# Three kinds of fp32 matmuls issued as halves in two column tiles of TensorE, in a macaron block with a gated delta rule

## The chip, the cores and the metric

The kernel runs as one program on one core of a Trainium2 chip. The metric is the device time of that core in microseconds (us). TensorE does the matmuls: it holds a stationary operand (the weights, at most 128 rows by 128 columns) and streams a moving operand of up to 512 columns past it, and it writes to PSUM, which has eight banks of 512 fp32 columns over 128 partitions. VectorE, ScalarE and GpSimd take the results out of PSUM and work on them, and SyncE issues the transfers (DMA). Each engine runs its own instructions in order and waits for others by semaphores.

## The reference

The input `x` has 8 sequences (B) of 512 positions (T) and 128 features (D). Three layers follow one another, each added to `x`:

```
x = x + 0.5 * ffn(layernorm(x))          # gated feed-forward, hidden 512
x = x + attn(layernorm(x))
x = x + 0.5 * ffn(layernorm(x))          # the same weights again

attn:  n = layernorm(x);  q = l2norm(silu(n @ Wq)); k = l2norm(silu(n @ Wk)); v = silu(n @ Wv)   # 8 heads of 128
       beta = sigmoid(n @ Wb); alpha = sigmoid(n @ Wa)
       S_t = a_t (I - b_t k_t k_t^T) S_{t-1} + b_t k_t v_t^T ;  o_t = S_t^T q_t                   # over t, for each head
       x = x + o @ Wo;  x = x + gelu(layernorm(x) @ W1 + b1) @ W2 + b2
```

All of it is in fp32.

## The kernel before

The recurrence over 512 positions is cut into 4 chunks (NC) of 128 positions. Within a chunk the products of keys with keys, masked and decayed, give a triangular matrix whose inverse is built by blocks (32, then 64, then 128), and a state of 128 x 128 for each of the 8 heads is carried from chunk to chunk. The eight sequences go through a software pipeline, written out by hand for each engine: while sequence s goes through its four chunks with the state, the projections and keys with keys of sequence p = s + 1 and the feed-forward layers of their neighbours stand between its pieces in TensorE's queue. Nothing is scheduled by a planner: the order in which the functions are called in `SP_first`, `SP_step` and `SP_last` is the order on TensorE.

These pieces of TensorE's program matter here:

- `proj(b, c, i)`, L1384 to L1391: one of the six projections (halves of 4 heads of q, k and v) of a chunk: stationary is `nT`, 128 x 128, moving a slice of `wqkv`, 128 x 512; it fills one bank (4 or 5). One matmul.
- `keys_keys(b, c, g)`, L1402 to L1415: for 4 heads (g = 0 or 1) the 128 x 128 product of the keys with themselves; stationary and moving are both `KT`. Four matmuls in bank 6 or 7, one column range each.
- `state_keys(b, c, g)`, L1432 to L1438: for 4 heads the keys with the state; stationary `KT`, moving `state`, 128 x 128. Four matmuls in bank 0 or 1.
- `join_one`, L1698 to L1716, called by `join`: the block inverse. It works with 32 x 32 and 64 x 64 pieces that lie in other rows (SBUF partitions of the operands) and other columns (PSUM partitions of the result) of the array. `join` issues two sides in turn; side 0 writes to bank 6, side 1 to bank 7. In step 3 (L1715 and L1716) both sides read partitions 32 to 63, one writes to partitions 0 to 31 and one to 32 to 63. In steps 5 and 8 (L1706 alone, L1707 alone) both sides lie in the same 64 x 64 tile.
- Full-array matmuls around them: the feed-forward layers L1284 (512 moving columns) and L1292 (128), the solve L1446, the queries with the state L1463, the update L1454, the output L1473, the attention's output L1482. L1384 is a small product with 32 stationary and 128 moving columns, over all 128 rows.

One step of `SP_step` issues in this order: `state_keys`, 2 projections, `solve`, `state_queries`, `update`, `keys_keys`, 2 projections, `output`, 2 projections, `attend`. The first sequence has its own functions for projections and keys with keys (`proj0`, `keys_keys0`: L1582, L1611), which the change leaves alone.

Of the kernel before, what the change touches and what calls it, by code (L numbers as in the profile page):

```python
# [52 lines left out]
def place(b, c, i):  # L53

    return ALONE.index((c, i)) if b == 0 else 6 * c + STEP_ORDER.index(i)


def at_end(b, c):

    return (b, c) == (B - 1, NC - 1)  # L60


def build_program(nc, d):
# [3 lines left out]
    with ctx:  # L67
        def sb(name, shape, dt=f32):
            return ctx.enter_context(nc.sbuf_tensor(name, shape, dt))

        def sem(name):
            return ctx.enter_context(nc.semaphore(name))
# [7 lines left out]
        wqkv = sb("wqkv", [128, 3, H * 128])  # L80
# [28 lines left out]
        nT = sb("nT", [128, T])  # L109
# [15 lines left out]
        KT = sb("KT", [128, U, 128])  # L125
# [6 lines left out]
        state = sb("state", [128, H, 128])  # L132
# [34 lines left out]
        bank = [ctx.enter_context(nc.psum_tensor(f"bank{i}", [128, 512], f32)) for i in range(8)]  # L167

        def heads(bk):
            return bk[:, :].rearrange("p (h n) -> p h n", h=4)  # L170
# [70 lines left out]
        p_proj, p_silu = sem("p_proj"), sem("p_silu")  # L241
# [1032 lines left out]
        def _(pe):  # L1274
# [111 lines left out]
            def proj(b, c, i):  # L1386
                n = place(b, c, i)
                if n >= 2:
                    pe.wait_ge(p_silu, b * 6 * NC + n - 1)
                pe.matmul(bank[4 + n % 2][:, :], nT[:, 128 * c:128 * c + 128], wqkv[:, i // 2, 512 * (i % 2):512 * (i % 2) + 512],  # L1390
                          start=True, stop=True).then_inc(p_proj, 1)  # L1391

            def turn(b, c, g):

# [7 lines left out]
            def keys_keys(b, c, g):  # L1402

                if at_end(b, c):
                    pe.wait_ge(p_trc, 4 * NC + g + 1)
                elif g == 0:
                    pe.wait_ge(k_in[c % 2], 16 * NBLK * (2 * (b - 1) + c // 2 + 1))
                if c > 0:
                    pe.wait_ge(p_dk, b * 2 * NC + 2 * c - 1 + g)
                else:  # L1410
                    pe.wait_ge((j_dve, j_act)[g], b * NS)
                for h in range(4):
                    u = H * c + 4 * g + h
                    last = pe.matmul(heads(bank[6 + g])[:, h, :], KT[:, u, :], KT[:, u, :], start=True, stop=True)  # L1414
                last.then_inc(p_kk, 1)  # L1415

            def keys_queries(b, c, g):
# [14 lines left out]
            def state_keys(b, c, g):  # L1432

                pe.wait_ge(s_S, b * 6 + 2 * (c - 1) + g + 1)
                for h in range(4):
                    u = H * c + 4 * g + h
                    last = pe.matmul(heads(bank[g])[:, h, :], KT[:, u, :], state[:, 4 * g + h, :], start=True, stop=True)  # L1437
                last.then_inc(s_ks, 1)  # L1438

            def solve(b, c, g):  # L1440
# [44 lines left out]
            def SP_first(s, p):  # L1485

                pe.wait_ge(j_dve, s * NS + AHEAD)
                pe.wait_ge(j_act, s * NS + AHEAD)
                if p is not None:
                    pe.wait_ge(n_bias, s + 2)  # L1490
                solve(s, 0, 0), solve(s, 0, 1)
                early = p is None or p == 1
                if not early:
                    pe.wait_ge(F["f1"]["sc"], p + 1)
                    pe.wait_ge(F["f2"]["sc"], p)
                    proj(p, 0, 2), proj(p, 0, 3)
                join(s, AHEAD, JOIN_BANKS)
                update(s, 0, 0)
                if not early:
                    proj(p, 0, 0)  # L1500
                update(s, 0, 1)
                if not early:
                    proj(p, 0, 1)
                join_waits(s, AHEAD + 1)
                output(s, 0, 0), output(s, 0, 1)
                join(s, AHEAD + 1, JOIN_BANKS)
                if p is not None:
                    proj(p, 0, 4), proj(p, 0, 5)
                attend(s, 0)

            def SP_step(s, p, c, f1):

                state_keys(s, c, 0), state_keys(s, c, 1)
                if p is not None:
                    proj(p, c, 2), proj(p, c, 3)
                if c < 3:
                    pe.wait_ge(j_act, s * NS + AHEAD + c)
                    pe.wait_ge(j_dve, s * NS + AHEAD + c)
                solve(s, c, 0), solve(s, c, 1)
                state_queries(s, c, 0), state_queries(s, c, 1)  # L1520
                if c < NC - 1:
                    update(s, c, 0), update(s, c, 1)
                elif p is not None:
                    proj(p, c, 0), proj(p, c, 1)
                if p is not None:
                    keys_keys(p, c - 1, 0), keys_keys(p, c - 1, 1)
                if c < NC - 1 and p is not None:
                    proj(p, c, 0), proj(p, c, 1)
                output(s, c, 0), output(s, c, 1)
                if p is not None:  # L1530
                    proj(p, c, 4), proj(p, c, 5)
                    if c == NC - 1 and f1 is not None:
                        input_T("f1", f1)
                    if at_end(p, c):
                        turn(p, c, 0), turn(p, c, 1)
                attend(s, c)

            def SP_last(s, p, f1):

                if f1 is None and p is not None:  # L1540
                    keys_keys(p, NC - 1, 0), keys_keys(p, NC - 1, 1)
                if f1 is not None:
                    layer1("f1", f1, 0)
                    pe.wait_ge(s_xa, s * NC + NC)
                    layer1("f1", f1, 1), layer1("f1", f1, 2), layer1("f1", f1, 3)
                    keys_keys(p, NC - 1, 0), keys_keys(p, NC - 1, 1)
                    pe.wait_ge(F["f1"]["silu"], f1 * KB + 3)
                pe.wait_ge(ln_m.rows, s + 1)
                transposes(xa, m_tr)
                if f1 is not None:  # L1550
                    pe.wait_ge(p_silu, p * 6 * NC + 6 * NC)
                else:
                    pe.wait_ge(s_xa, s * NC + NC)
                    M_up(s, None), M_down(s, p)
                    if p is not None:
                        keys_queries(p, 0, 0), keys_queries(p, 0, 1)
# [230 lines left out]
```

## Time and profile before

| | |
|---|---|
| median of 2 runs | 1490.54 us (1488.46 to 1492.62) |
| the profiled execution, its own time | 1489.32 us |
| its span, first to last instruction | 1487.6 us |
| mean granted TensorE clock | 0.982 of full speed |
| TensorE busy | 1418.9 us (95%) |
| VectorE, ScalarE, GpSimd busy | 820.9 (55%), 668.6 (45%), 564.9 us (38%) |

The profile is of one execution. "PE" is TensorE's matmuls and "PEld" its weight loads, which can lie beneath matmuls; the recorded length of a matmul holds its way through the array, so it is longer than the distance from one to the next. The chain of waits goes back from the last instruction to what released it, each time; its pieces have the distances between instructions, not their recorded lengths. L1390 and the like are lines of the kernel. An engine's idle time counts only if it lies on that chain.

### The profile page before, as it was taken

Reading aid. Unit: us, or ns where it says so; the run is one execution under the profiler, and the core shown is the slowest. Engines: PE = TensorE matmul, PEld = TensorE weight load, DVE = VectorE, ACT = ScalarE, POOL = GpSimd, SP = SyncE. Lnnn points to the kernel's source line nnn. Section 1 sums busy time; section 2 is a strip of 40 time slices with the busy share of each in tenths; the row PEclk is TensorE's granted clock in tenths of the full one; section 3 lists DMA queues with packets and bytes.
Section 4 is the critical chain, followed back from the end, with each engine's and each line's share of the span. In section 5 each row is a group of like instructions: output and inputs, shape, how many; then the busy total and the mean of one; then the engine's idle time right before and its main releaser. Section 6 shows DMA issues by size and latency. Waiting matters only on the chain.

```text
span 1487.6 us, 25821 instructions
## 1 busy us (share of the span) xinstructions
PE 1418.9 (95%) x10118; PEld 966.2 (65%) x10118; DVE 820.9 (55%) x2432; ACT 668.6 (45%) x1130; POOL 564.9 (38%) x641
## 2 busy tenths in 40 slices
PE   7998899999999999999999999999999999889968
PEld 3455776557866587557865588566875578656934
DVE  3467387454865367644764557753776437641330
ACT  2466466225652356325562256523563256512222
POOL 0038042831447133650428314471336504381000
PEclk9999899999999999999999999999999999989979
DMA  5130244532454135630455325641356304543000
GB/s 173 42 100 29 41 104 116 108 82 65 122 115 99 34 88 130 132 82 23 104 123 102 82 65 122 111 106 31 92 126 124 82 23 111 112 77 76 1 0 7
DMA packets 359546, 125.04 MB, mean 84 GB/s; under 512 B 325280, under 2 KB 340352, under 8 KB 359424
## 3 DMA queue, kind: packets, MB, share of 16 engines
q1 hardware_dynamic: 359424, 123.38, 36.2%
q8 instruction: 80, 1.31, 0.3%
q14 instruction: 42, 0.34, 0.1%
HBM read 79.58 MB, written 43.76 MB: 83 GB/s over the span
## 4 chain that ended last, share of the span: by engine, by line
PE 89%; DVE 7%; ACT 1%; DMA 1%; SPq 1%; issue 1%; DVEq 0%; ACTq 0%
PE bank L1284 29%; PE bank L1390 9%; PE bank L1313 5%; PE bank L1292 4%; PE bank L1446 4%; PE bank L1473 4%; PE bank L1482 4%; PE bank L1429 3%; PE bank L1414 3%; PE bank L1454 3%; PE bank L1463 3%; PE bank L1437 3%; PE bank L1706 2%; PE bank L1671 2%; PE bank L1680 2%; PE bank L1715 1%
## 5 line engine op out<-in xcount | busy, mean ns | idle before, releaser
L1284 PE MATMUL bank<-big,h 128*128 128x512 f32 x992 | 447.1, 596 | 0.0
L1284 PEld LDWEIGHTS bank<-big,h 128*128 128x128 f32 x992 | 181.6, 190 | 197.0 <-issue 192.5
L512 POOL TENSOR_TENSOR rnorm<-ssq,mhalf 128x16 f32<-128x16 f32 (+1 forms) x35 | 84.0, 2401 | 516.8 <-DVE ssq L773 516.8
L1390 PE MATMUL bank<-wqkv,nT 128*128 128x512 f32 x336 | 160.2, 596 | 0.0
L558 POOL TENSOR_TENSOR blkT<-blkT,blkP 128x31 f32<-128x31 f32 (+15 forms) x248 | 135.8, 547 | 19.4
L555 POOL TENSOR_TENSOR blkP<-blkA,blkT 128x31 f32<-128x31 f32 (+15 forms) x248 | 129.2, 521 | 31.1 <-DMA blkA<-blocks_out 12.3
L1313 PE MATMUL bank<-xT,w 128*128 128x512 f32 x256 | 122.7, 626 | 8.4 <-ACT xT L1038 4.2
L908 DVE TENSOR_SCALAR TB<-bank 32x512 f32<-32x512 f32 (+1 forms) x48 | 33.1, 689 | 153.0 <-PE bank L1713 74.3
L1055 ACT ACTIVATE big<-bank,cols 128x512 f32<-128x512 f32 x64 | 43.0, 686 | 138.3 <-PE bank L1284 100.4
L887 DVE TENSOR_TENSOR MT<-bank,MT 128x512 f32<-128x512 f32 x56 | 38.6, 691 | 104.3 <-PE bank L1429 104.3
L1313 PEld LDWEIGHTS bank<-xT,w 128*128 128x128 f32 x256 | 49.0, 201 | 66.5 <-issue 50.9
L1062 ACT ACTIVATE big<-bank,cols 128x512 f32<-128x512 f32 x64 | 43.1, 686 | 108.6 <-PE bank L1284 108.5
L521 POOL TENSOR_TENSOR MT<-rows_or_g,maskf 128x1024 f32<-128x1024 f32 x28 | 78.2, 2792 | 11.5 <-PE bank L1473 11.0
L539 POOL TENSOR_TENSOR QET<-QET,sgf 128x1024 f32<-128x1024 f32 x21 | 49.3, 2350 | 86.7 <-DMA sgf<-e_rows 86.7
L1390 PEld LDWEIGHTS bank<-wqkv,nT 128*128 128x128 f32 x336 | 56.8, 191 | 37.4 <-issue 36.8
L1124 ACT ACTIVATE MT<-MT,biasj 128x128 f32<-128x128 f32 x256 | 78.2, 389 | 0.3
L1446 PEld LDWEIGHTS bank<-V,R 128*128 128x128 f32 x512 | 63.0, 196 | 15.0 <-issue 12.5
L1429 PEld LDWEIGHTS bank<-QET,KT 128*128 128x128 f32 x448 | 58.4, 197 | 20.4 <-issue 14.4
L1292 PE MATMUL bank<-w,big 128*128 128x128 f32 x512 | 68.2, 279 | 2.3 <-DVE TB L908 1.5
L1292 PEld LDWEIGHTS bank<-w,big 128*128 128x128 f32 x512 | 62.6, 192 | 11.8 <-issue 8.4
L1134 ACT ACTIVATE big<-bank 128x512 f32<-128x512 f32 x56 | 32.7, 597 | 82.8 <-PE bank L1390 82.7
L1446 PE MATMUL bank<-V,R 128*128 128x128 f32 x512 | 64.7, 281 | 3.7 <-DVE V L915 2.1
(213 smaller groups left out, 2598.6 us busy)
## 6 DMA issues: line engine op xcount, KB each, us to landing
rows_or_g<-g_rows SPq DMA_DIRECT2D x28, 512.0 KB, 4.9
q_rows<-mid SPq DMA_DIRECT2D x28, 512.0 KB, 4.9
QET<-q_rows SPq DMA_DIRECT2D x112, 128.0 KB, 4.2
k_rows<-R SPq DMA_DIRECT2D x27, 512.0 KB, 2.7
KT<-k_rows SPq DMA_DIRECT2D x108, 128.0 KB, 3.6
sgf<-e_rows SPq DMA_DIRECT2D x21, 512.0 KB, 4.6
blocks_out<-R SPq DMA_DIRECT2D x128, 32.0 KB, 1.7
blkA<-blocks_out SPq DMA_DIRECT2D x8, 512.0 KB, 3.8
```

The costliest lines, as they stand in the source:

```text
L512: pool.tensor_tensor(rnorm[:, heads_of], ssq[:, heads_of], mhalf[:, :].to_broadcast([128, heads_of.stop - heads_of.start]), ALU.pow).then_ ...
L521: pool.tensor_tensor(MT[:, u, :], grow, maskf[:, :].unsqueeze(1).to_broadcast([128, H, 128]), ALU.add).then_inc(d_mask, 1)
L555: pool.tensor_tensor(prod, A3[:, j, j + 1:].unsqueeze(2).to_broadcast([128, n, m]), T3[:, j:j + 1, 0:m].to_broadcast([128, n, m]), ALU.mul ...
L558: pool.tensor_tensor(T3[:, j + 1:, 0:m], T3[:, j + 1:, 0:m], prod, ALU.subtract).then_inc(b_prod, 1)
L1124: last = act.activation(MT[:, u, :], MT[:, u, :], ACT.Exp, bias=biasj[:, u:u + 1])
L1284: last = pe.matmul(bank[bk + i][:, :], w[:, k, 128 * o:128 * o + 128], src[:, k, :], start=(k == 0), stop=(k == KB - 1))
L1292: last = pe.matmul(bank[4][:, 128 * c:128 * c + 128], src[:, k, 128 * c:128 * c + 128], w[:, k, :], start=(k == 0 and c == 0), stop=(k == ...
L1313: pe.matmul(bank[bk][:, :], w[:, 128 * o:128 * o + 128], xT[:, :], start=True, stop=True).then_inc(f["gate"], 1)
L1390: pe.matmul(bank[4 + n % 2][:, :], nT[:, 128 * c:128 * c + 128], wqkv[:, i // 2, 512 * (i % 2):512 * (i % 2) + 512], start=True, stop=True ...
L1429: last = pe.matmul(heads(bank[6 + g])[:, h, :], KT[:, u, :], QET[:, u, :], start=True, stop=True)
L1446: last = pe.matmul(heads(bank[g])[:, h, :], R[:, u, :], V[:, u, :], start=True, stop=True)
L1473: last = pe.matmul(heads(bank[2 + g])[:, h, :], V[:, u, :], MT[:, u, :], start=(c == 0 and h == 0), stop=True, skip_group_check=True)
```

## The change

In `proj`, the 128 stationary columns are issued as two matmuls of 64 columns, the first writing to PSUM partitions 0 to 63 and the second to 64 to 127; the moving operand of 512 columns is streamed by both. `state_keys` is cut in the same way, in turn for each head. In `keys_keys` the stationary and the moving columns are both halved, so that each head has four matmuls of 64 x 64 with the two partition halves in turn. The semaphore is raised by the last matmul only, as before.

```diff
--- before.py
+++ after.py
@@ -1387,8 +1387,10 @@
                 n = place(b, c, i)
                 if n >= 2:
                     pe.wait_ge(p_silu, b * 6 * NC + n - 1)
-                pe.matmul(bank[4 + n % 2][:, :], nT[:, 128 * c:128 * c + 128], wqkv[:, i // 2, 512 * (i % 2):512 * (i % 2) + 512],
-                          start=True, stop=True).then_inc(p_proj, 1)
+                for half in (slice(0, 64), slice(64, 128)):
+                    last = pe.matmul(bank[4 + n % 2][half, :], nT[:, 128 * c + half.start:128 * c + half.stop],
+                                     wqkv[:, i // 2, 512 * (i % 2):512 * (i % 2) + 512], start=True, stop=True)
+                last.then_inc(p_proj, 1)
 
             def turn(b, c, g):
 
@@ -1411,7 +1413,9 @@
                     pe.wait_ge((j_dve, j_act)[g], b * NS)
                 for h in range(4):
                     u = H * c + 4 * g + h
-                    last = pe.matmul(heads(bank[6 + g])[:, h, :], KT[:, u, :], KT[:, u, :], start=True, stop=True)
+                    for half in (slice(0, 64), slice(64, 128)):
+                        for part in (slice(0, 64), slice(64, 128)):
+                            last = pe.matmul(heads(bank[6 + g])[part, h, half], KT[:, u, part], KT[:, u, half], start=True, stop=True)
                 last.then_inc(p_kk, 1)
 
             def keys_queries(b, c, g):
@@ -1434,7 +1438,8 @@
                 pe.wait_ge(s_S, b * 6 + 2 * (c - 1) + g + 1)
                 for h in range(4):
                     u = H * c + 4 * g + h
-                    last = pe.matmul(heads(bank[g])[:, h, :], KT[:, u, :], state[:, 4 * g + h, :], start=True, stop=True)
+                    for half in (slice(0, 64), slice(64, 128)):
+                        last = pe.matmul(heads(bank[g])[half, h, :], KT[:, u, half], state[:, 4 * g + h, :], start=True, stop=True)
                 last.then_inc(s_ks, 1)
 
             def solve(b, c, g):
```

TensorE's queue in one step of the recurrence (`SP_step`, from the end of `attend` to the next `attend`). A row is a run of the same instruction: line, operation, bank written, operands, columns written by partitions and moving columns, number. Before:

```order
L1482 MATMUL bank<-wo,blkA 128x128 x8
L1437 MATMUL bank<-state,KT 128x128 x8
L1390 MATMUL bank<-wqkv,nT 128x512 x2
L1446 MATMUL bank<-V,R 128x128 x8
L1463 MATMUL bank<-QET,state 128x128 x8
L1454 MATMUL bank<-V,KD 128x128 x8
L1414 MATMUL bank<-KT 128x128 x8
L1390 MATMUL bank<-wqkv,nT 128x512 x2
L1473 MATMUL bank<-MT,V 128x128 x8
L1390 MATMUL bank<-wqkv,nT 128x512 x2
```

The same piece now (lines behind the change have moved by up to five):

```order
L1487 MATMUL bank<-wo,blkA 128x128 x8
L1442 MATMUL bank<-state,KT 64x128 x16
L1391 MATMUL bank<-wqkv,nT 64x512 x4
L1451 MATMUL bank<-V,R 128x128 x8
L1468 MATMUL bank<-QET,state 128x128 x8
L1459 MATMUL bank<-V,KD 128x128 x8
L1418 MATMUL bank<-KT 64x64 x32
L1391 MATMUL bank<-wqkv,nT 64x512 x4
L1478 MATMUL bank<-MT,V 128x128 x8
L1391 MATMUL bank<-wqkv,nT 64x512 x4
```

No piece has changed its place. Three unbroken runs of halved matmuls (L1442 with L1391, L1418 with L1391, L1391) now stand between groups that use the full array.

The start of a sequence (`SP_first`), where projections stand next to a join of 64 x 64 tiles (L1707, now L1712). Before:

```order
L1473 MATMUL bank<-MT,V 128x128 x8
L1707 MATMUL bank<-R,TB 64x64 x16
L1390 MATMUL bank<-wqkv,nT 128x512 x2
L1482 MATMUL bank<-wo,blkA 128x128 x8
L1437 MATMUL bank<-state,KT 128x128 x8
```

Now:

```order
L1478 MATMUL bank<-MT,V 128x128 x8
L1712 MATMUL bank<-R,TB 64x64 x16
L1391 MATMUL bank<-wqkv,nT 64x512 x4
L1487 MATMUL bank<-wo,blkA 128x128 x8
L1442 MATMUL bank<-state,KT 64x128 x16
```

Here the halves stand between the join's tiles and the full array, where the full array followed the join at once.

## Rows read from the trace of the kernel before

**Rows 1.** The page: span, busy time of each engine, the chain by engine.

```profile
span 1487.6 us, 25821 instructions
PE 1418.9 (95%) x10118; PEld 966.2 (65%) x10118; DVE 820.9 (55%) x2432; ACT 668.6 (45%) x1130; POOL 564.9 (38%) x641
...
PE 89%; DVE 7%; ACT 1%; DMA 1%; SPq 1%; issue 1%; DVEq 0%; ACTq 0%
```

**Rows 2.** Windows: busy us of each engine in two stretches.

```profile
core 0: us, PE busy (x) PEld busy (x) DVE busy (x) ACT busy (x) POOL busy (x), PEclk, DMA share, GB/s
200.00:1080.00 880.00, 876.11 (x6351) 598.54 (x6352) 524.19 (x1531) 411.20 (x684) 374.34 (x403) 1.00 0.42 93
1080.00:1300.00 220.00, 212.76 (x1510) 149.26 (x1509) 132.54 (x385) 111.34 (x191) 92.55 (x90) 0.98 0.42 96
```

**Rows 3.** Groups by line: count, busy us, mean ns, idle before.

```profile
L1390 PE MATMUL bank<-wqkv,nT 128*128 128x512 f32 x336 | 160.2, 596 | 0.0
...
L1414 PE MATMUL bank<-KT 128*128 128x128 f32 x448 | 54.7, 275 | 1.5 <-DMA KT<-k_rows 1.5
...
L1437 PE MATMUL bank<-state,KT 128*128 128x128 f32 x384 | 46.8, 275 | 0.0
```

**Rows 4.** Chain of waits, one step: start us, us, what, passes.

```profile
556.13 1.79 PE bank L1437 x16
557.91 1.72 PE bank L1390 x4
...
564.99 1.79 PE bank L1414 x16
...
570.28 1.72 PE bank L1390 x4
...
573.78 1.79 PE bank L1437 x16
```

**Rows 5.** The chain where the shape of the tile changes.

```profile
492.46 3.63 PE bank L1284 x8
...
514.75 0.89 PE bank L1292 x8
515.65 2.00 PE bank L1706 x32
517.65 1.09 PE bank L1292 x8
...
519.11 0.34 PE bank L1384 x2
519.44 1.09 PE bank L1292 x8
520.53 0.20 PE bank L1706
...
607.02 3.43 PE bank L1284 x8
```

**Rows 6.** Timeline of TensorE, joins: start us, recorded us, line, rows*columns, moving.

```profile
505.99 0.21 PE L1715 MATMUL bank<-R,TB 32*32 32x32 f32 x1
505.99 0.21 PE L1716 MATMUL bank<-TB,R 32*32 32x32 f32 x1
...
506.99 0.19 PE L1715 MATMUL bank<-R,TB 32*32 32x32 f32 x1
...
520.46 0.27 PE L1706 MATMUL bank<-TB,R 64*64 64x64 f32 x1
520.47 0.27 PE L1707 MATMUL bank<-R,TB 64*64 64x64 f32 x1
...
520.57 0.22 PE L1706 MATMUL bank<-TB,R 64*64 64x64 f32 x1
520.57 0.22 PE L1707 MATMUL bank<-R,TB 64*64 64x64 f32 x1
...
520.74 0.22 PE L1706 MATMUL bank<-TB,R 64*64 64x64 f32 x1
```

## The prediction

> **What bounds the kernel now.** I read the page first: the profiled execution took 1489.32 us, its span is 1487.6 us, TensorE is busy 95% of it and the chain that ended last is 89% TensorE [rows 1]. The table of windows then says where: from 200 to 1080 us TensorE is busy 876.1 of 880 us at full clock (2.4 GHz); VectorE, the next engine, 524.2 [rows 2]. Whatever is added to TensorE's queue in this stretch is added to the time, nearly one for one. The groups by line give the counts: L1390 (projections) x336 for 168 matmuls, L1414 (keys with keys) x448 for 224, L1437 (keys with state) x384 for 192 [rows 3]: every fp32 matmul runs as two passes, each with its weight load. The chain through one step gives what a pass costs when the queue is full: L1390 x4 in 1.72 us, 0.43 a pass of 512 columns; L1414 and L1437 x16 in 1.79 us, 0.112 a pass of 128 columns [rows 4]. The loads are hidden beneath the pass before.
>
> **What the change does to the passes.** It takes no multiplication away. Each matmul becomes two with 64 stationary columns, or four for keys with keys, whose moving side is halved too.
>
> *Projections:* 2 tiles x 2 passes of 512 moving columns for each matmul. If the two tiles run side by side, the pair takes what one pass took, 0.43: change 0. One after the other: 168 x 2 x 0.43 = +144 us.
>
> *Keys with state:* 2 tiles x 2 passes of 128 moving columns; side by side 0.112 per pair of passes, change 0; in turn 24 groups (192 matmuls by 8) x 1.79 = +43. A gain would need a pass of 128 moving columns to be shorter with lighter weights. L1384, with 32 stationary and 128 moving columns, excludes it: x2 takes 0.34, of which the first carries 0.12 for the switch, so 0.11 a pass [rows 5].
>
> *Keys with keys:* 8 matmuls become 32, which is 64 passes of 64 x 64. L1706 shows such a pass inside one tile, x32 in 2.00, and L1706 with L1707 in two tiles, a pair each 0.058 (rows of the chain give 0.05 or 0.06; from 520.57 to 520.74 there are three steps of 0.057) [rows 5, 6]. Side by side: 32 x 0.058 = 1.86 instead of 1.79, +0.07 x 28 groups = +2 us. In turn: 64 x 0.058 = 3.7, +1.9 x 28 = +54.
>
> Whether two tiles that read the *same* rows run side by side is the first thing to settle. L1715 and L1716 at 506 us are such a case: both read partitions 32 to 63 and write to different partitions. 64 passes start between 505.99 and 506.99, in pairs 0.01 apart and 0.032 from pair to pair [rows 6]. A pass of 64 columns takes 0.058, so one of 32 can hardly take 0.016: they do overlap, weight loads included. I take side by side as the value.
>
> **The term that is left: switches of tile shape.** Rows 5 show it at every join. L1292 x8 takes 0.89 behind another full-array group and 1.09 behind a join; L1284 x8 takes 3.43 and 3.63: entering the full array costs **0.20**. The first pair of a 64 x 64 join takes 0.20 against 0.058, L1706 x32 takes 2.00 against 32 x 0.058 = 1.86: entering 64-wide tiles costs **0.14**. It is not a matter of rows: L1384 keeps all 128 rows and only narrows the columns to 32, pays 0.34 - 2 x 0.11 = 0.12 to enter, and L1292 x8 behind it takes 1.09 again [rows 5]. So the full array and the two column tiles are to be expected to pay too, and the weight load that is hidden otherwise (64 columns going in, 128 coming out) lies open at each.
>
> How often is in the order of the two programs, counted over all of TensorE's matmuls. The halved ones stand in 101 unbroken runs: 49 of projections alone, 21 of keys with state and projections, 21 of keys with keys and projections, 7 of keys with keys and 3 of keys with state. So there are 101 new entries into the column tiles (92 from the full array, 7 from the 64 x 64 joins, 2 from the 32 x 32 ones). Entries into the full array rise from 80 to 166; those into the join tiles stay 32 and 40. The sum: 101 x 0.14 = 14.1, and 86 x 0.20 = 17.2, **31.3 us**. For the unseen shape (128 rows, 64 columns) I take 0.14, since the load that lies open has 64 columns as in L1706; the ends are 0.12 (L1384) and 0.20 (as for a full load), and 0.19 to 0.20 for the way out: 28.5 to 37.4 us.
>
> **What hides some of it.** Between 200 and 1300 us TensorE idles 11.1 us in all, 7.2 of them after 1080 [rows 2]; most of it follows TensorE's own transposes, so it moves along and hides nothing. One early run stands ahead of a wait for VectorE, and a few steps in the latency-bound first 200 us have slack. I take off 1 us, at most 3. No DMA or other engine is added to, and all that wait for TensorE get their data later, not earlier. No buffer comes free sooner, so nothing new is triggered.
>
> **Sum:** 1489.3 + 31.3 + 2 - 1 = 1521.6, call it **1522 us**. The median of the runs is 1490.5, 1.2 above the profiled execution; 1522 is 2.1% over it. Its own range is 1489.3 + 28.5 + 2 - 3 = 1517 to 1489.3 + 37.4 + 2 = 1529.
>
> **The rivals.**
>
> *A, the switch between the full array and its two column tiles is free.* It ends on the other side, at no change. The mechanism: all 128 rows stay in use and the same two operand streams run, so the engine need not empty, and the first 64-column load slips under the last pass. Price: +2 for keys with keys, 1491 us. For it: no row shows just this shape. Against: L1384 narrows only columns and pays both ways [rows 5]. It decides from the point where entry and exit together are under 0.31, since then 94 round trips make less than 2% (29.8 us, less keys with keys). Chance 0.09.
>
> *B, the tiles do not run side by side,* because both stream the same operand at full depth and write to one PSUM bank, which the joins never do (their two sides write to two banks). So the change would not do what it says. Price 144 + 43 + 54 = 241 more: 1762 us. Against: L1715 with L1716 [rows 6]. Chance 0.09.
>
> *C, the passes stay in strict order.* The program issues both passes of one tile, then both of the other. In strict order the second tile's first pass starts only with the first tile's second, and each run is one slot longer: about 91 runs with a projection x 0.43 = 39 us, 1561 us. The rows speak against it: 520.57 shows L1706 and L1707 both at their second pass, and at 505.99 both tiles start at once [rows 6]. The order of issue differs from the order of start. The Trainium skill has the rule from which C comes, "TensorE: Matmul & The Clock Gate", Part 3: matmuls start and end in program order, and only weight loads are pulled ahead. By that rule it would be 1561 us; this trace disagrees with it where tiles differ (L1706 and L1707 0.01 us apart). Chance 0.05.
>
> One more rule of the Trainium skill speaks against this change, in the same page and part: weight loads overlap matmuls in flight only where the row group differs (or the load goes to the background weights). Both column tiles have all the row groups. If each load lay open, the time would go towards B. The trace has L1715 and L1716 in one row group at 0.032 a pair, load included, so I give this no chance beyond B's.
>
> **The numbers.** Forecast 0.75 (1517 to 1529), A 0.09, B 0.09, C 0.05; 0.02 stays for a gain that no row explains. A measurement of this kernel can tell about 2% from no change, which is 1520.4 us. Of the forecast's 0.75, 0.47 lies above the line and 0.28 below. Slower by over 2%: 0.47 + 0.09 + 0.05 = 0.61. Within: 0.28 + 0.09 = 0.37. Faster: 0.02. The range goes down to A and a little past the forecast's upper end: 1490 to 1538, which holds 0.73 + 0.09 = 0.82.
>
> **What would show it.** In the profile after: L1391 x672 with pairs of rows 0.01 apart and four pairs in 1.72 us (right), or x8 in 3.44 (B), or a first row that stands alone for 0.43 (C). The full-array group behind a run of halves x16 in 1.98 instead of 1.78 or 1.79, and each run of halves 0.14 longer: a step that took 17.65 us (from L1437 to L1437, [rows 4]) takes 18.7 (three runs, 3 x 0.34). Keys with keys x64 in 1.86 to 2.0. If the full-array groups behind a run stay at 1.78, A holds. The prediction is wrong above all if a pair of 512-column passes over all rows takes more than 0.43: each 10% on it costs 14 us.

## Result, and the profile after

| | before | changed |
|---|---|---|
| median, first runs | 1490.54 us | 1521.28 us (1520.92 to 1521.63) |
| median, runs of a later session (13 and 4) | 1492.58 us | 1523.88 us |
| ratio of that session | | 1.0216, interval 1.0191 to 1.0241 |
| span of the profiled execution | 1487.6 us | 1519.9 us |
| TensorE busy | 1418.9 us | 1450.6 us |

The halves cost 31 us (2.1%), as forecast (1522). The ratio of the first runs was 1.0206 with a 95% interval of 1.0144 to 1.0268; the later one puts the change at +32 us, 28.5 to 36. Where a run is put at so many us over before, that is its ratio less one, times the median of before in its own session; intervals are of 95%. The runs of one kernel lie up to 8 us from their median (1488.14 to 1499.88 us for the kernel before in one session), so profiles are compared by pieces more than by spans. One run of the version in blocks of four below took 1891.74 us at a granted clock of 0.742 and is in none of the figures.

The page of the changed kernel, what answers to [rows 1], and its groups for [rows 3]:

```profile
span 1519.9 us, 29949 instructions
PE 1450.6 (95%) x12182; PEld 953.3 (63%) x12182; DVE 823.0 (54%) x2432; ACT 669.9 (44%) x1130; POOL 557.5 (37%) x641
...
L1391 PE MATMUL bank<-wqkv,nT 128*64 128x512 f32 x672 | 163.8, 605 | 0.0
...
L1418 PE MATMUL bank<-KT 128*64 128x64 f32 x1792 | 58.0, 223 | 1.9 <-DMA KT<-k_rows 1.9
L1442 PE MATMUL bank<-state,KT 128*64 128x128 f32 x768 | 47.2, 276 | 0.0
```

TensorE has 31.7 us more of busy time, and VectorE and ScalarE have what they had. Twice the passes for the projections (x672 for x336) have left their busy time nearly alone (160.2 before, 163.8 now).

The chain of waits through one step, for [rows 4] (start us, us, line, number of passes):

```profile
569.90 1.90 PE bank L1442 x32
571.80 1.72 PE bank L1391 x8
573.51 1.98 PE bank L1451 x16
575.50 1.79 PE bank L1468 x16
577.28 1.79 PE bank L1459 x16
579.07 2.02 PE bank L1418 x64
581.09 1.72 PE bank L1391 x8
582.80 1.98 PE bank L1478 x16
584.79 1.87 PE bank L1391 x8
586.65 1.98 PE bank L1487 x16
588.63 1.46 PE bank L1442 x23
```

From L1442 to L1442 it is 18.73 us, where before had 17.65 from L1437 to L1437 and 18.7 was forecast. Read it by what stands in front. L1391 x8 takes 1.72 behind other halves, just what x4 took before, and 1.87 behind the full array (+0.15). The full-array groups L1451, L1478 and L1487 take 1.98 behind a run of halves (+0.20), and L1468 and L1459, which stand behind other full-array groups, still 1.79.

The +0.20 has two parts, which the starts of single passes show (TensorE's timeline at the first pass of L1451: start us, recorded us, "PEld" its weight load):

```profile
572.92 0.60 PE L1391 MATMUL bank<-wqkv,nT 128*64 128x512 f32 x2
573.44 0.19 PEld L1451 LDWEIGHTS bank<-V,R 128*128 128x128 f32 x1 [0.81 <-issue]
573.45 0.38 PE L1451 MATMUL bank<-V,R 128*128 128x128 f32 x1
```

This pass starts 0.53 behind the last pair of halves, whose 512 columns take 0.43: some 0.09 go by with neither. Its weights, which are loaded beneath the pass before where the shape stays, are loaded only now, and it is recorded for 0.38 where the same pass of the kernel before (L1446) had 0.27: 0.10 for the load that lies open. Why the 0.09 go by is not shown.

The whole of a sequence can be read from the first group of L1671 (now L1676), which comes once in each. Before:

```profile
603.58 3.43 PE bank L1671 x8
...
776.91 3.43 PE bank L1671 x8
```

Changed:

```profile
441.96 3.43 PE bank L1676 x8
...
619.85 3.43 PE bank L1676 x8
```

173.33 us have become 177.89: +4.56 for each sequence, by 14 runs of halves and 12 more entries into the full array (14 x 0.14 + 12 x 0.20 + 4 x 0.07 = 4.64 by the prediction's prices).

### The profile page after: what moved, and what is told of

Its sections match the earlier page's. It is cut to its first block, busy times and chain, and to the rows that moved or that the text cites. A ratio compares the mean times of both kernels' runs of the same rounds, so it can differ in the third digit from the quotient of the medians.

```text
span 1519.9 us, 29949 instructions
## 1 busy us (share of the span) xinstructions
PE 1450.6 (95%) x12182; PEld 953.3 (63%) x12182; DVE 823.0 (54%) x2432; ACT 669.9 (44%) x1130; POOL 557.5 (37%) x641
## 4 chain that ended last, share of the span: by engine, by line
PE 87%; DVE 7%; POOL 3%; issue 2%; ACT 1%; DMA 1%; SPq 0%; DVEq 0%; POOLq 0%; ACTq 0%
PE bank L1284 28%; PE bank L1391 10%; PE bank L1313 5%; PE bank L1292 4%; PE bank L1451 4%; PE bank L1478 4%; PE bank L1487 4%; PE bank L1418 4%; PE bank L1459 3%; PE bank L1433 3%; PE bank L1442 3%; PE bank L1468 3%; PE bank L1711 2%; PE bank L1676 2%; PE bank L1685 2%
## 5 line engine op out<-in xcount | busy, mean ns | idle before, releaser
L1391 PE MATMUL bank<-wqkv,nT 128*64 128x512 f32 x672 | 163.8, 605 | 0.0
L1313 PE MATMUL bank<-xT,w 128*128 128x512 f32 x256 | 119.2, 611 | 8.8 <-DVE big L674 4.6
L1313 PEld LDWEIGHTS bank<-xT,w 128*128 128x128 f32 x256 | 47.4, 195 | 64.8 <-issue 48.1
L521 POOL TENSOR_TENSOR MT<-rows_or_g,maskf 128x1024 f32<-128x1024 f32 x28 | 70.0, 2501 | 23.9 <-PE bank L1478 23.9
L1451 PEld LDWEIGHTS bank<-V,R 128*128 128x128 f32 x512 | 61.5, 196 | 21.7 <-issue 13.4
L1391 PEld LDWEIGHTS bank<-wqkv,nT 128*64 128x64 f32 x672 | 41.4, 137 | 50.1 <-issue 44.0
L1451 PE MATMUL bank<-V,R 128*128 128x128 f32 x512 | 67.0, 285 | 3.5 <-DVE V L915 2.0
```

The lines of the kernel that those rows point to most:

```text
L521: pool.tensor_tensor(MT[:, u, :], grow, maskf[:, :].unsqueeze(1).to_broadcast([128, H, 128]), ALU.add).then_inc(d_mask, 1)
L1313: pe.matmul(bank[bk][:, :], w[:, 128 * o:128 * o + 128], xT[:, :], start=True, stop=True).then_inc(f["gate"], 1)
L1391: last = pe.matmul(bank[4 + n % 2][half, :], nT[:, 128 * c + half.start:128 * c + half.stop], wqkv[:, i // 2, 512 * (i % 2):512 * (i % 2) ...
L1451: last = pe.matmul(heads(bank[g])[:, h, :], R[:, u, :], V[:, u, :], start=True, stop=True)
```

## The experiments

Theory S is the prediction's: the passes cost what they did, and every switch of tile shape costs 0.14 us going into the column tiles and 0.20 going into the full array. The rivals differ from run to run. The changed kernel was run again (its ratio stands in the table):

> The changed kernel once more, against the kernel before in the same session. Both theories: 31 us slower (1.021), since it is the same program; the run narrows the interval, which was 1.014 to 1.027.

### One kind of matmul at a time

Each of these three takes one of the diff's three hunks and leaves the other two out.

> Only the projections are issued as halves; keys with keys and keys with state stay whole. Theory S (each switch of tile shape costs 0.14 us into column tiles and 0.20 into the full array): 91 entries into column tiles and 156 instead of 80 into the full array, 91 x 0.14 + 76 x 0.20 = +28 us, nearly all of the whole change's 31. Rival M (each added matmul costs the same, 31 us by 1032 added ones, 0.03 each): 168 added, +5 us.

> Only keys with keys are cut, in four. S: 28 entries into column tiles and 28 more into the full array, 28 x 0.34 = 9.5, and 2 for the passes of 64 columns: +11.5 us. M: 672 added matmuls, 65% of all that the change adds, +20 us.

> Only keys with state are halved. S: 24 entries each way, 24 x 0.34 = +8 us. M: 192 added matmuls, +6 us. The three parts together: S expects 28 + 11.5 + 8 = 47.5, which is more than the whole change costs, because runs that touch share their switches; M expects the parts to add up to the whole, 31.

| halved | entries into column tiles / more into the full array | expected by S | by M | ratio (interval) | measured |
|---|---|---|---|---|---|
| projections | 91 / 76 | +28 | +5 | 1.0187 (1.0162 to 1.0212) | +27.9 us |
| keys with keys | 28 / 28 | +11.5 | +20 | 1.0073 (1.0045 to 1.0101) | +10.9 us |
| keys with state | 24 / 24 | +8 | +6 | 1.0039 (1.0021 to 1.0056) | +5.8 us |
| sum of the three | 143 / 128 | 47.5 | 31 | | 44.6 us |
| all three at once | 101 / 86 | 31 to 33 | 31 | 1.0216 (1.0191 to 1.0241) | +32.2 us |

The cost goes by the switches, not by the added matmuls: 168 added ones cost 27.9 us and 672 cost 10.9. The parts add up to more than the whole, as runs that touch share their switches. The smallest part is under what S expected. Its chain shows why:

```profile
577.40 1.90 PE bank L1438 x32
579.30 1.91 PE bank L1390 x4
```

The entry costs 0.11 here and the exit 0.19 (L1390 x4 took 1.72 before): 24 x 0.30 = 7.2. The entry is 0.15 less a little that comes back: 16 pairs of narrow passes take 0.109 each and 16 whole ones 0.112.

### A switch without any halved work

```diff
+                if i % 2 == 0:
+                    pe.matmul(bank[4 + n % 2][0:64, 0:1], nT[:, 128 * c:128 * c + 64], wqkv[:, i // 2, 0:1], start=True, stop=True)
                 pe.matmul(bank[4 + n % 2][:, :], nT[:, 128 * c:128 * c + 128], wqkv[:, i // 2, 512 * (i % 2):512 * (i % 2) + 512],
```

and its control, the same with all 128 stationary columns (`bank[4 + n % 2][:, 0:1]`, `nT[:, 128 * c:128 * c + 128]`).

> The kernel before, with all its matmuls whole, and one needless matmul of 64 stationary and 1 moving column ahead of each first projection of a pair (84 places); the projection overwrites its result. Theory S (the switch of shape is what costs): entry 0.14, two passes that are as long as their weight loads (2 x 0.058), exit 0.20: 0.45 each, 84 x 0.45 = +38 us. Theory P (the halved passes cost, not the switch): only the two passes, 84 x 0.12 = +10 us.

> The control for the tiny matmul: the same 84 needless matmuls of 1 moving column with 128 stationary columns, so the array's shape never changes. Both theories: two passes as long as a load of 128 columns (0.11), 84 x 0.22 = +19 us. S: some 20 us less than with the narrow one, though it loads twice the weights. P: some 9 us more than with the narrow one.

The narrow one came to 1522.20 us, ratio 1.0189 (1.0161 to 1.0216), +28 us; the full one to 1510.27, 1.0114 (1.0090 to 1.0137), +17. The sign decides for S: half the weights cost 11 us more, where P expected 9 less. The size is smaller than expected (28 for 38, and 11 for 20). The chain of the narrow one:

```profile
572.06 0.21 PE bank L1391 x2
572.26 1.91 PE bank L1392 x4
```

and of the control:

```profile
566.32 0.12 PE bank L1391 x2
566.44 1.82 PE bank L1392 x4
```

0.21 + 0.19 = 0.40 a place instead of 0.45: the load of the first pass is the one that the entry leaves open, and I had counted it in both. The control is 0.12 + 0.10 = 0.22, as expected. The way out was counted too often as well: 8 of the 84 places stand behind a join (7 behind 64 x 64 tiles, 1 behind 32 x 32), where the kernel before had paid its 0.20 already, so there are 76 new entries into the full array. The rows then give 84 x 0.40 - 8 x 0.20 = 32 us for the narrow one, at the upper end of its interval (24 to 32), and 84 x 0.18 - 8 x 0.20 = 13.5 for the difference; 11 were measured, within the two intervals.

### How far ahead a tile's passes are taken

In keys with keys and keys with state the loop over the column tile was made the outermost one:

```diff
-                for h in range(4):
-                    u = H * c + 4 * g + h
-                    for half in (slice(0, 64), slice(64, 128)):
+                for half in (slice(0, 64), slice(64, 128)):
+                    for h in range(4):
+                        u = H * c + 4 * g + h
```

(shown for `state_keys`; `keys_keys` likewise, with the output's partition half outermost).

> The changed kernel, but keys with keys and keys with state issue all of one column tile's matmuls of 4 heads first (8 or 16 passes), then all of the other's; projections as in the change. Theory Q (each tile takes its passes from the queue on its own, as far ahead as this): no difference to the change, +31 us over before. Rival F (the look-ahead is short, a few passes): the second tile waits while the first works, so up to 8 x 0.112 = 0.9 us for each of the 48 groups of keys with state and 16 x 0.058 = 0.9 for each of the 56 of keys with keys, up to 94 us more: +125 us over before.

1572.88 us, ratio 1.0532 (1.0504 to 1.0560), +80 us: both were wrong, and the truth lies between. Windows over L1442 alone tell how many of its passes start in the first 0.45 us (the number in brackets behind the first busy time, which is that of the matmuls), tile by tile:

```profile
569.35:569.80 0.45, 0.44 (x4) 0.45 (x5) 1.00 0.00 0
```

and in the changed kernel, tiles in turn:

```profile
569.82:570.27 0.45, 0.44 (x8) 0.44 (x10) 1.00 0.32 50
```

Four passes run alone, and only then does the other tile join in. By the starts in the trace it is the same at every later change of tile, also from one group to the next and to the projections behind: the last 4 passes of a tile run beside the first 4 of the next tile, and no more than that. With 8 passes a tile, only the first 4 of each two groups are alone; with 16 (keys with keys) it is 12 of the first tile and 8 in the middle of each of the other three. The price agrees with the chain:

```profile
569.43 2.17 PE bank L1442 x29
571.60 0.11 PE bank L1391
571.71 0.22 PE bank L1442 x2
```

This is 2.50 us for a pair of groups instead of 1.90. The 0.60 are 4 x 0.11 for the passes alone and three times some 0.05 for the weight load that lies open where a tile joins in. For L1418 the same rows add up to 3.34 (3.16, 0.06 and 0.12) instead of 2.02: 24 x 0.60 + 28 x 1.32 = 51 us on top of the change's 32, so 83 by the rows for 80 measured. Each time three passes of the first tile were still waiting when the second tile's first one started. Blocks of 4 passes should then lose nothing:

```diff
+                for pair in (0, 2):
+                    for half in (slice(0, 64), slice(64, 128)):
+                        for h in (pair, pair + 1):
```

(shown for `state_keys`; in `keys_keys` the loops over `half` and `part` change places).

> The changed kernel with the tiles in turn by blocks of 4 passes instead of 2, for keys with keys (both halves of the moving side, then the other tile) and keys with state (two heads, then the other tile). In the run that issued tile by tile, the second tile's first pass started with the 5th of 8 passes of the first for keys with state, and with the 13th of 16 for keys with keys: each time three passes of the first tile were still waiting in front of it. Theory L (a pass is taken past three waiting ones of another tile): with blocks of 4 the second tile starts with the first, and the time is that of the change, +31 us over before. Rival (the look-ahead is shorter than three, or it loses part of a block): 1 to 2 passes lost for each block, 0.1 to 0.2 for each two heads of keys with state, so 10 to 20 us more, and likewise for keys with keys.

Ratio 1.0222 (1.0192 to 1.0252), +33 us, so as the change. Its groups hardly lose anything, 0.04 and 0.05 over those of the change, 2.3 us in all:

```profile
585.08 2.06 PE bank L1418 x64
...
594.69 1.95 PE bank L1443 x32
```

So the rule read from the one run foretold the other: a tile's pass starts past at most three waiting ones of another tile. That a fourth is not passed was seen with passes of 64 and of 128 columns. With passes of 512 columns, three are passed too (the next experiment), and a fourth was not tried. Whether the limit counts the passes or their instructions (each has its weight load) these runs can't tell.

### Four column tiles

```diff
-                for half in (slice(0, 64), slice(64, 128)):
+                for half in (slice(0, 32), slice(32, 64), slice(64, 96), slice(96, 128)):
```

(in `proj`, the other two kinds whole).

> Projections in four column tiles of 32 stationary columns, the rest whole; to be held against the one with projections in halves. Theory S with four tiles side by side: the same 91 entries, each some 0.02 cheaper, since the load that lies open has 32 columns instead of 64 (0.12 instead of 0.14): +26 us over before against +28 for halves. Rival (only two operand streams at a time): 168 x 2 x 0.43 = 144 more, +172 us.

1517.33 us, ratio 1.0160 (1.0137 to 1.0183), +24 us against 28 for halves; the intervals overlap, and the chain shows the 0.02:

```profile
562.25 1.85 PE bank L1391 x16
564.11 1.98 PE bank L1484 x16
```

Sixteen passes of 512 columns take 1.85 us, with the entry: four full-depth streams run side by side. TensorE's timeline at the entry (window 562.15 to 562.30) has all four tiles started within it:

```profile
562.18 0.64 PE L1391 MATMUL bank<-wqkv,nT 128*32 128x512 f32 x4
```

The program issues two passes of each tile, so the fourth tile's first pass starts past the waiting second passes of the other three. The way out costs the same 0.20, since the load that lies open there is the full array's.

### Fewer switches by another order

```diff
                 if c < NC - 1:
                     update(s, c, 0), update(s, c, 1)
-                elif p is not None:
-                    proj(p, c, 0), proj(p, c, 1)
-                if p is not None:
-                    keys_keys(p, c - 1, 0), keys_keys(p, c - 1, 1)
-                if c < NC - 1 and p is not None:
-                    proj(p, c, 0), proj(p, c, 1)
                 output(s, c, 0), output(s, c, 1)
+                if p is not None:
+                    keys_keys(p, c - 1, 0), keys_keys(p, c - 1, 1)
+                    proj(p, c, 0), proj(p, c, 1)
```

> The kernel before with the order of a step changed: output ahead of keys with keys, so that keys with keys and four projections stand together; all matmuls whole. The number of switches is that of the kernel before (80 into the full array). It is the base for the next one. Expected at 1490 plus what the last two projections wait for ScalarE to empty their banks, 0 to 20 us; in the step before the change of order they had output between them and had time.

> The same order with all three kinds halved. The order takes 21 runs of halves away: 80 entries into column tiles instead of 101, 145 into the full array instead of 166. Theory S: 80 x 0.14 + 65 x 0.20 + 2 = +26 us over the same order with whole matmuls, against +31 to 33 for the original order; if that order has waits of its own, part of the 26 may lie beneath them. Rival M (the cost is in the 1032 added matmuls): +31 us over it, as before.

Whole: 1496.88 us, 1.0031 (1.0015 to 1.0046), +4.6. Halved: 1514.77, 1.0165 (1.0139 to 1.0191), +24.6. The new order takes 7.6 us off the halved kernel (32.2 to 24.6, from two sessions with some 4 us of uncertainty each; by S 21 x 0.34 = 7.1). Over its own base the halved one costs 20 us, not 26. One sequence takes, with whole matmuls,

```profile
604.19 3.43 PE bank L1668 x8
...
772.40 2.05 PE bank L1414 x16
...
778.33 3.43 PE bank L1668 x8
```

and with halves

```profile
612.88 3.43 PE bank L1673 x8
...
789.94 3.43 PE bank L1673 x8
```

174.14 and 177.06, against 173.33 before. One sequence has 11 runs of halves, and 9 more entries into the full array than before: 11 x 0.14 + 9 x 0.20 + 4 x 0.07 = 3.6 by S over before, and 3.73 are measured. So the new order by itself makes waits of 0.8 a sequence, and with halves most of them lie beneath the switches. Two kinds can be seen in the base, in the waits of this stretch (us in total, times, longest):

```profile
PEld bank L1390 <- ACT QET L1134: 3.7, 6, 0.7
...
PE bank L1414 <- DMA KT<-k_rows: 0.3, 1, 0.3
```

The last keys with keys wait for the transfer of their keys. TensorE's timeline there, before and in the base:

```profile
769.80 1.45 PE L1313 MATMUL bank<-xT,w 128*128 128x512 f32 x3
771.09 1.17 PE L1414 MATMUL bank<-KT 128*128 128x128 f32 x9
...
770.69 1.45 PE L1313 MATMUL bank<-xT,w 128*128 128x512 f32 x3
772.40 0.82 PE L1414 MATMUL bank<-KT 128*128 128x128 f32 x5 [0.26 <-DMA KT<-k_rows]
```

L1414 starts 1.71 behind that row of L1313 instead of 1.29, so 0.42 late, and by the starts in the trace its first pass takes 0.10 more. The rest is ScalarE, which I had named: weight loads of the projections wait for it to empty a bank. It shows in the three places of a sequence where four projections stand in a row (L1390 x8 in 3.53 instead of 3.44), together 0.3. With halves the keys come 0.04 late by the same starts (L1418 starts 0.56 behind the last pass of L1313, and 0.52 in the changed kernel of the old order), and four projections take 3.50 where two behind other halves take 1.72:

```profile
576.49 3.50 PE bank L1391 x16
```

So of the 0.8 some 0.2 stay, ScalarE's part for the most, and the switches cover the wait for the keys.

### A version faster than both

The kernel before has switches of its own. The cheapest to remove is that of L1384:

```diff
-        lga = sb("lga", [128, U])
+        lgaw = sb("lgaw", [128, 128])
+        lga = lgaw[:, 0:U]
...
+            pool.memset(lgaw[:, U:], 0.0)
...
-                pe.matmul(logit_bank(b)[0:U, 4 * U:4 * U + C], lga[:, :], triu[:, :], start=True, stop=True).then_inc(n_g, 1)
+                pe.matmul(logit_bank(b)[:, 4 * U:4 * U + C], lgaw[:, :], triu[:, :], start=True, stop=True).then_inc(n_g, 1)
```

> The kernel before with one switch of shape less in each sequence: the product of L1384 with 32 stationary columns is issued with 128 (96 zero columns behind the 32), so that it stays in the full array's shape. Theory S: L1384 x2 0.22 instead of 0.34 and the group behind it 0.20 shorter, 8 x 0.32 = 2.6 us faster than before, 0.17%; in the chain L1292 x8 takes 0.89 there instead of 1.09. Rival (the narrow product's cost is in its own way through the array): no difference.

1488.87 us (12 runs) against 1491.82 (17), ratio 0.9976 (0.9963 to 0.9989): 3.6 us faster, 1.6 to 5.5, so faster by 0.1 to 0.4%. Its chain:

```profile
518.98 0.22 PE bank L1385 x2
519.21 0.30 PE bank L1386 x2
519.51 0.89 PE bank L1294 x8
```

The group behind takes 0.89 instead of 1.09, as expected. But the product itself takes 0.30, not 0.22, though nothing switches any more: a place gains 0.24, 1.9 us in eight. TensorE's timeline tells why, before and in this version:

```profile
518.72 0.39 PE L1383 MATMUL bank<-lga,ones 128*128 128x32 f32 x2
519.04 0.41 PE L1384 MATMUL bank<-triu,lga 128*32 128x128 f32 x2
...
518.82 0.39 PE L1385 MATMUL bank<-lgaw,ones 128*128 128x32 f32 x2
519.04 0.47 PE L1386 MATMUL bank<-triu,lgaw 128*128 128x128 f32 x2
```

The product starts 0.32 behind the two short passes of L1383 before, and 0.22 behind them now, so some 0.09 of the narrow product's 0.34 were the switch. What the wide product loses again is its own load: its two passes are recorded for 0.06 more (0.47 for 0.41), since it has 128 columns of weights to load where the narrow one had 32, and behind passes as short as L1383's that load isn't hidden.

## Why the prediction was right

*What bounds the kernel.* Right. TensorE is busy 31.7 us more, the span is 32.3 us longer, and the busy time of the other engines has not grown by more than 2.1 us.

*The passes cost nothing.* Right, for the reason given. L1391 x8 in 1.72 settles rival B, and four tiles in the same time do it once more. The unseen conditions (one PSUM bank, all 128 rows, the same moving operand) make no difference that shows.

*0.14 in, 0.20 out, 101 and 86 times.* The exit was exact (1.98 for 1.78). The entry was 0.15 for the 56 runs that begin with projections, 0.11 for the 24 that begin with keys with state, and 0.23 for the 21 that begin with keys with keys, 0.07 of it the work of shorter passes that I had counted by itself. With 0.08 more for the 7 keys with keys inside a run: 8.4 + 2.6 + 4.8 + 0.6 + 86 x 0.20 = 33.6. The sum had 33.3 before it took 1 us off for what waits hide; the span grew by 32.3. That it comes out to 0.1 us of the forecast's 32.3 is partly luck: the single prices were off by up to 0.03, in both directions, and the 1 us was a guess that no run checks by itself.

*The reading of L1384.* I took 0.12 of its 0.34 as the switch. The padded product gains only 0.04, which seems to speak against it, but its row has a full weight load lying open that the narrow one had not. By the starts, the 0.12 are 0.09 for the switch, and the rest is the short load of its 32 columns, so the reading stands, and with it the proof that narrowing the columns alone costs a switch; the group behind it (1.09 for 0.89) says the same. The sentence that a pass of 128 moving columns gets no shorter with lighter weights used the 0.11 that it was to prove. The changed kernel has 0.109 for a pair of half-width passes and 0.112 for a whole one, so the gain is there, but it is only 0.04 to 0.05 us for 16 pairs.

*Rival A* (switching is free) fell with the 1.98 and with the tiny matmul. *Rival C* (strict order) fell: the second tile's pass overtakes the first's. But it was nearer to the truth than its 0.05 said of another kernel. The order is kept loosely, with three passes of freedom, and the change stays within that because it takes the tiles in turn at every matmul. Tile by tile it would have cost 50 us more. The rule of the Trainium skill, that matmuls start in program order ("TensorE: Matmul & The Clock Gate", Part 3), is not what these runs show between different tiles: the first passes of both tiles start together (L1391 in four tiles, x4 within 0.15 us), ahead of second passes that were issued earlier. The same Part 3 has a model in which packed tiles take the time of one plus some nanoseconds each; this trace agrees with it in L1391: its pairs take 0.43 as one did.

*What stays open.* That the change is slower is clear (the interval begins at 1.0191); that it is slower by over 2% is not, since that interval reaches below 1.02. The entry is 0.15 in front of projections and 0.11 in front of keys with state; the 16 pairs at 0.109 instead of 0.112 account for the difference, but no run varied their number. By the measured prices the sum is 33.6, and where the 1.3 us over the span's growth are hidden was not traced.

## What to carry to other kernels

Cut a matmul that fills the array into column tiles only for a reason other than speed: side by side the tiles take as long as the whole did, and each visit to another tile shape costs some 0.30 to 0.35 us here, in and out, in a queue that is full. Count the unbroken runs of each shape in the queue's order, not the matmuls. Group equal shapes, pad a lone small product to the shape around it, and where tiles must be used take them in turn within four passes. Padding pays less where the full weight load then lies open behind short passes.

## What the runs showed of the hardware

- Two and four column tiles over all 128 rows, which stream the same operand and write to one bank, run side by side: 1.72 us for 8 and 1.85 with the entry for 16 passes of 512 columns (4 took 1.72).
- A switch of tile shape costs 0.11 to 0.15 us into 64-column tiles and 0.19 to 0.20 into the full array, also when only the columns change. Of the latter 0.09 go by before the first pass of the new shape starts (0.53 behind a pair that takes 0.43), and 0.10 are that pass's weight load, which is not hidden (0.38 for 0.27 recorded).
- Passes of another tile start past waiting ones, up to three of them: in turn by 2 or 4 passes the tiles overlap wholly (1.90 and 1.95 us for 32 passes of 128 columns), by 8 the first 4 run alone and each later join costs some 0.05 (2.50 us), by 16 only 4 at each end overlap (3.34 instead of 2.02 us for 64 passes of 64 columns).
